# A graph layer with residual and layer norm on one Trainium2 core: pair counting of groups 1 to 3 regrouped from three turns to two, six pair places, the table word loaded inside the loop

## The reference

```python
agg = segment_sum(x[src], dst, num_segments=6250)          # 6250 x 256
h = relu(agg @ W_rel + b_rel + x @ W_root)                 # 6250 x 512
i, f, g, o = split(h @ W_ih.T + b_ih + b_hh, 4)            # f is not used
c = sigmoid(i) * tanh(g)
y = (sigmoid(o) * tanh(c)) @ W_fc + b_fc                   # 6250 x 256
out = layernorm(x + y)                                     # eps 1e-5
```

## Time and profile before

| | us |
|---|---|
| median of three runs | 1830.2 |
| profiled execution | 1824.41 |
| its span, first to last instruction | 1822.5 |
| TensorE matmuls busy | 1513.5 |
| GpSimd busy | 1281.0 |
| VectorE busy | 815.9 |
| ScalarE busy | 418.5 |
| mean granted TensorE clock | 0.91 of full |

### The profile page before, as it was taken

The page is one execution under the profiler, slowest core; times in us unless marked ns, Lnnn a source line. Parts: engine busy times, 40 slices in busy tenths (PEclk is TensorE's granted clock), DMA queues, the critical chain, the costliest instruction groups (busy, mean ns, idle before and its releaser), DMA issues.

```text
span 1822.5 us, 31499 instructions
## 1 busy us (share of the span) xinstructions
PE 1513.5 (83%) x6882; PEld 1213.0 (67%) x6883; DVE 815.9 (45%) x1763; ACT 418.5 (23%) x743; POOL 1281.0 (70%) x1926
## 2 busy tenths in 40 slices
PE   0157688697988898788998889899988888999997
PEld 0023355486767676667887667688876676888886
DVE  8877666431322654531324565422244654222332
ACT  0001021110112332220222333212223332222333
POOL 5875877777777877877777668776763668656640
PEclk9976677698988998889999999999998998999999
DMA  9563555576766555567766445576652455766540
GB/s 342 209 233 87 150 161 145 157 225 207 215 195 180 162 162 165 161 198 223 223 206 180 138 133 166 160 246 217 203 155 77 133 146 161 225 189 177 150 122 18
DMA packets 131966, 319.14 MB, mean 175 GB/s; under 512 B 17295, under 2 KB 68268, under 8 KB 130198
## 3 DMA queue, kind: packets, MB, share of 16 engines
q0 software_dynamic: 75264, 245.95, 46.4%
q10 hardware_dynamic: 52632, 54.80, 9.5%
q1 hardware_dynamic: 3936, 16.62, 2.4%
HBM read 298.10 MB, written 19.20 MB: 174 GB/s over the span
## 4 chain that ended last, share of the span: by engine, by line
PE 48%; POOL 21%; issue 19%; DVE 4%; DMA 3%; DVEq 3%; POOLq 1%; ACT 0%; ACTq 0%; SPq 0%
PE ps_blk L537 20%; POOL rows L400 14%; PE ps_agg L476 9%; PE ps_win L464 6%; POOL idx L370 6%; PE ps_y L545 4%; PE ps_blk L519 3%; PE ps_blk L524 3%; PE ps_tr L451 1%; DMA hot_key<-in_xb 1%; POOL rows L385 1%; PE ps_win L451 1%; DMA rows<-x_parts,idx 1%; POOLq L370 1%; DMA wih_sb<-in_x 1%
## 5 line engine op out<-in xcount | busy, mean ns | idle before, releaser
L400 POOL DMA_INDIRECT rows<-x_parts,idx x924 | 963.5, 1043 | 453.5 <-PE ps_agg L476 157.6
L537 PE MATMUL ps_blk<-cell,wih_sb 128*128 128x250 f32 x2400 | 545.5, 385 | 2.9 <-issue 2.2
L537 PEld LDWEIGHTS ps_blk<-cell,wih_sb 128*128 128x128 f32 x2400 | 464.1, 196 | 69.5 <-issue 8.8
L476 PE MATMUL ps_agg<-rows,onehot 128*125 x1112 | 341.8, 462 | 153.2 <-SPq L339 70.8
L476 PEld LDWEIGHTS ps_agg<-rows,onehot 128*125 128x125 f32 x1112 | 234.1, 216 | 227.5 <-issue 175.9
L906 DVE SCALAR_TENSOR_TENSOR onehot<-iota_f,tile_first,dst_u 128x500 f32 (+1 forms) x278 | 207.0, 746 | 291.7 <-PE ps_agg L476 171.6
L370 POOL COPY idx<-src_sb 128x1 int32 x956 | 264.4, 277 | 16.7 <-issue 9.7
L664 ACT ACTIVATE cell<-ps_blk,bg_sb 128x250 f32<-128x250 f32 x300 | 140.8, 470 | 544.0 <-PE ps_blk L537 470.2
L897 DVE TENSOR_TENSOR hot_key<-iota_h,rel 128x980 f16 x263 | 174.4, 663 | 0.4 <-issue 0.4
L464 PE MATMUL ps_win<-adj,hot_key 128*128 128x250 f32 x784 | 170.7, 375 | 2.4 <-DMA hot_key<-in_xb 1.5
L464 PEld LDWEIGHTS ps_win<-adj,hot_key 128*128 128x128 f32 x784 | 148.0, 190 | 21.6 <-DMA hot_key<-in_xb 4.0
(11 more groups left out here) (125 smaller groups left out, 914.2 us busy)
## 6 DMA issues: line engine op xcount, KB each, us to landing
hot_key<-in_xb ACTq DMA_DIRECT2D x28, 896.0 KB
rows<-x_parts,idx POOLq DMA_INDIRECT x924
x_t<-in_xT ACTq DMA_DIRECT2D x25, 250.0 KB
x_n<-in_x ACTq DMA_DIRECT2D x25, 250.0 KB
out<-y ACTq DMA_DIRECT2D x25, 250.0 KB
x_parts<-wih_sb SPq DMA_DIRECT2D x4, 1024.0 KB, 6.8
wih_sb<-in_x ACTq DMA_DIRECT2D x6, 512.0 KB, 9.7
x_parts<-cell SPq DMA_DIRECT2D x2, 1024.0 KB, 7.6
```

Of the source, the lines that this page charges most:

```text
L400: g.indirect_dma_start(rows_f[:, k * QC + j, :], None, x_parts, bass.IndirectOffsetOnAxis(ap=idx[:, k, j:j + 1], axis=0)).then_inc(landed[ ...
L476: ins = mm(o, onehot[:, hot * QC + j, 0:TN], rows[:, ds(slot + j, 1), :].squeeze(1), start=(first and j == 0), stop=False)
L537: last = mm(o, wih_sb[:, k, col:col + P], h_t[:, k, :], start=(k == 0), stop=(k == KH - 1))
```

## The change

`SLOTS` becomes (3, 3, 3, 3), so groups 1 to 3 are dealt as group 0 is: 3, 3, 3, 3 and 3, 3, 3, 4 windows in two turns. Turns 5 and 6 count group 1, 7 and 8 multiply, 9 is group 1; groups 2 and 3 follow in 10 to 14 and 15 to 19. Turn 20 sums the second tile of group 20, turns 21 to 24 are plain. Pair places are six instead of four, the table has one more (zero) word. The table word of the next span is loaded inside the pair loop of the present one; the first before all loops. Memory for the larger places comes from `src_sb`: the int32 sources now land in the last place of `rows` (`src_i`), VectorE makes a 16-bit copy `src_u` for GpSimd, and the first gather into that place waits until VectorE has read the int32 words (`src_read`).

```diff
--- before.py
+++ after.py
@@ -17,7 +17,7 @@
 GROUP_WINDOWS = GN // WN
 WINDOWS = DENSE * GROUP_WINDOWS
 SPANS = DENSE * GN // SN
-FIRST_SLOTS, SLOTS = (3, 3, 3, 3), (2, 2, 3, 2)
+FIRST_SLOTS, SLOTS = (3, 3, 3, 3), (3, 3, 3, 3)
 SRC_HI = -(-N_NODES // P)
 SCOLS = SN * SRC_HI
 WCOLS = WN * SRC_HI
@@ -32,7 +32,7 @@
 MAX_STEPS = TILES * (STEPS - 1) + 1
 MAX_VISITS = TILES * STEPS
 MAX_PAIRS = SPANS * STEPS
-PAIRS = 4
+PAIRS = 6
 QP, QPC = 98, 16
 RING = 7
 IDX_AHEAD = 1
@@ -55,7 +55,7 @@
 
 
 T_MORE_A, T_MORE_B, T_STEPS, T_GROUP0, T_SPAN = 0, 64, 128, 129, 160
-T_COLS = T_SPAN + SPANS
+T_COLS = T_SPAN + SPANS + 1
 PACK = 2048
 
 
@@ -148,7 +148,7 @@
         ident = sb("ident", [P, P])
         ones = sb("ones", [P, 1])
         zero_bf = sb("zero_bf", [P, 256], bf16)
-        src_sb = sb("src_sb", [P, CHUNK_COLS], i32)
+        src_u = sb("src_u", [P, CHUNK_COLS], u16)
         dst_u = sb("dst_u", [P, CHUNK_COLS], u16)
         src_lo = sb("src_lo", [P, CHUNK_COLS], f16)
         key = sb("key", [P, CHUNK_COLS], u16)
@@ -191,6 +191,7 @@
         flat = rows_f.rearrange("p r d -> p (r d)")
         dstq_sb = flat[0:QP, 0:QPC * CHUNK].bitcast(i32).rearrange("p (c e) -> p c e", c=QPC)
         dst_next = flat[0:QP, QPC * CHUNK:(QPC + 1) * CHUNK].bitcast(i32)
+        src_i = flat[:, (RING - 1) * QC * D_ROW:(RING - 1) * QC * D_ROW + CHUNK_COLS].bitcast(i32)
         cell_flat = cell[:, :, :].rearrange("p i n -> p (i n)")
         wih_flat = wih_sb[:, :, :].rearrange("p k n -> p (k n)")
         flat_a = adj[:, :, :].rearrange("p k n -> p (k n)")
@@ -240,6 +241,8 @@
 
         dstq_in = sem("dstq_in")
         edges_in = sem("edges_in")
+        src_short = sem("src_short")
+        src_read = sem("src_read")
         bias_in = sem("bias_in")
         weights_in = sem("weights_in")
         piece_in = [sem(f"piece_in{i}") for i in range(X_PIECES)]
@@ -294,9 +297,11 @@
         steps_begun = sem("steps_begun")
         stats_seen = sem("stats_seen")
 
-        def unpack(engine, regs, at):
+        def load_span(engine, regs, at):
+            engine.reg_load(regs[0], table[0:1, at:at + 1] if isinstance(at, int) else table[0:1, ds(at, 1)])
+
+        def unpack(engine, regs):
             packed, first, past = regs
-            engine.reg_load(packed, table[0:1, at:at + 1] if isinstance(at, int) else table[0:1, ds(at, 1)])
             engine.reg_alu(first, packed, PACK, ALU.python_divide)
             engine.reg_alu(past, first, -PACK, ALU.mult)
             engine.reg_add(past, past, packed)
@@ -314,7 +319,7 @@
         def _(sp):
             sp.dma_start(dstq_sb, dstq[0:QP * QPC * CHUNK].rearrange("(p c e) -> p c e", p=QP, c=QPC)).then_inc(dstq_in, 16)
             sp.dma_start(dst_next, dstq[QPC * CHUNK:(QP + 1) * QPC * CHUNK].rearrange("(p e) -> p e", p=QP)[:, 0:CHUNK]).then_inc(dstq_in, 16)
-            sp.dma_start(src_sb[:, :], srcT).then_inc(edges_in, 16)
+            sp.dma_start(src_i, srcT).then_inc(edges_in, 16)
             sp.dma_start(dst_i, dstT).then_inc(edges_in, 16)
             sp.sem_inc(gathered, RING)
             for i in SP_PIECES:
@@ -359,7 +364,7 @@
                 pool.wait_ge(piece_high, i + 1)
                 g.tensor_tensor(low, low, piece(i)[:, :, 0, :], ALU.subtract).then_inc(piece_split_pool, 1)
             pool.wait_ge(table_ready, 1)
-            pool.wait_ge(edges_in, 32)
+            pool.wait_ge(src_short, 1)
             steps = pool.value_load(table[0:1, T_STEPS:T_STEPS + 1], min_val=2 * TILES, max_val=MAX_STEPS)
             group0 = pool.value_load(table[0:1, T_GROUP0:T_GROUP0 + 1], min_val=0, max_val=2 * STEPS)
 
@@ -367,7 +372,7 @@
                 return pool.snap(((s + group0) % STEPS) * QC, min_val=0, max_val=(STEPS - 1) * QC)
 
             def copy_index(chunk, k, j):
-                g.tensor_copy(idx[:, k % RING, j:j + 1], src_sb[:, ds(chunk + j, 1)]).then_inc(idx_copied, 1)
+                g.tensor_copy(idx[:, k % RING, j:j + 1], src_u[:, ds(chunk + j, 1)]).then_inc(idx_copied, 1)
 
             for k in range(IDX_AHEAD):
                 chunk = chunk_of(pool.snap(0 * steps + k))
@@ -381,6 +386,8 @@
                     for j in range(QC):
                         pool.wait_ge(landed[ahead - RING][j], 16)
                 pool.sem_inc(steps_begun, 1)
+                if k == RING - 1:
+                    pool.wait_ge(src_read, 2)
                 for j in range(QC):
                     g.indirect_dma_start(
                         rows_f[:, k * QC + j, D_IN:D_ROW], None, x,
@@ -426,6 +433,7 @@
             place = pe.alloc_register("place")
             more_places = pe.alloc_register("more_places")
             pe.reg_mov(place, 0)
+            load_span(pe, pe_regs, T_SPAN)
             pe.reg_mov(step_0, 0)
             pe.reg_mov(visit_0, 0)
             pe.reg_mov(pair_0, 0)
@@ -442,7 +450,7 @@
                     for side in range(2):
                         at = w * 2 + (T_SPAN + side)
                         o = bank[:, side * SCOLS:(side + 1) * SCOLS]
-                        first, past = unpack(pe, pe_regs, at)
+                        first, past = unpack(pe, pe_regs)
                         with pe.Fori(first, past, QC):
                             s = pe.snap(pair_0, min_val=0, max_val=MAX_PAIRS)
                             half = pe.snap(place, min_val=0, max_val=PAIRS - 1)
@@ -450,6 +458,7 @@
                             for j in range(QC):
                                 last = mm(o, hot_lo[:, ds(half, 1), j // 2, :, j % 2].squeeze(1), hot_key[:, ds(half, 1), j // 2, :, j % 2].squeeze(1), start=False, stop=False)
                             last.then_inc(pairs_summed, 1)
+                            load_span(pe, pe_regs, at + 1)
                             next_pair(pe, pair_0, place, more_places)
                     marker(bank[:, 0:WCOLS]).then_inc(win_done, 1)
 
@@ -838,6 +847,8 @@
             link(v.tensor_scalar(row[:, BAD, 0:1], row[:, BAD, 0:1], 1.0, plain, ALU.add, ALU.mult))
             link(v.tensor_tensor(table[:, T_STEPS:T_STEPS + 1], row[:, BAD, 0:1], row[:, FLAG, 4:5], ALU.add))
             dve.sem_inc(table_ready, 1)
+            dve.wait_ge(edges_in, 32)
+            v.tensor_copy(src_u[:, :], src_i).then_inc(src_short, 1)
             split_pieces(POOL_PIECES, PARTS)
             count_below(SPANS, 2 * TILES + 1, (span_first[0:QP, :], span_end[0:QP, :]))
             dve.sem_inc(span_counts, 1)
@@ -855,12 +866,12 @@
             link(v.tensor_scalar(hi, hi, -float(QC - 1), None, ALU.add))
             link(v.scalar_tensor_tensor(table[:, T_SPAN:T_SPAN + SPANS], lo, float(PACK), hi, ALU.mult, ALU.add))
             dve.sem_inc(spans_ready, 1)
-            dve.wait_ge(edges_in, 32)
             v.tensor_copy(dst_u[:, :], dst_i).then_inc(setup, 1)
-            v.tensor_scalar(src_part, src_sb[:, :], P - 1, None, ALU.bitwise_and).then_inc(setup, 1)
-            v.tensor_scalar(src_high, src_sb[:, :], P.bit_length() - 1, None, ALU.logical_shift_right).then_inc(setup, 1)
-            n_setup[0] += 3
+            v.tensor_scalar(src_part, src_i, P - 1, None, ALU.bitwise_and).then_inc(src_read, 1)
+            v.tensor_scalar(src_high, src_i, P.bit_length() - 1, None, ALU.logical_shift_right).then_inc(src_read, 1)
+            n_setup[0] += 1
             dve.wait_ge(setup, n_setup[0])
+            dve.wait_ge(src_read, 2)
             link(v.tensor_copy(src_lo[:, :], src_part))
             link(v.tensor_scalar(wide, dst_u[:, :], float(DENSE * GN), float(SRC_HI), ALU.min, ALU.mult))
             link(v.tensor_tensor(key[:, :], wide, src_high, ALU.add))
@@ -874,6 +885,7 @@
             place = dve.alloc_register("place")
             more_places = dve.alloc_register("more_places")
             dve.reg_mov(place, 0)
+            load_span(dve, dve_regs, T_SPAN)
             step_0 = dve.alloc_register("step_0")
             visit_0 = dve.alloc_register("visit_0")
             pair_0 = dve.alloc_register("pair_0")
@@ -884,7 +896,7 @@
             def span(w, side):
                 at = w * 2 + side
                 static = isinstance(w, int)
-                first, past = unpack(dve, dve_regs, at + T_SPAN)
+                first, past = unpack(dve, dve_regs)
                 with dve.Fori(first, past, QC) as c:
                     s = dve.snap(pair_0, min_val=0, max_val=MAX_PAIRS)
                     half = dve.snap(place, min_val=0, max_val=PAIRS - 1)
@@ -893,6 +905,7 @@
                                     None, ALU.subtract).then_inc(rel_made, 1)
                     v.tensor_tensor(hot_lo[:, ds(half, 1), :, :, :].squeeze(1), iota_h[:, 0:P, :].unsqueeze(1).to_broadcast([P, PQ, P, 2]),
                                     src_lo[:, ds(c, QC)].rearrange("p (q c) -> p q c", c=2).unsqueeze(2).to_broadcast([P, PQ, P, 2]), ALU.is_equal)
+                    load_span(dve, dve_regs, at + (T_SPAN + 1))
                     dve.wait_ge(rel_made, s + 1)
```

## The result

The changed kernel takes 1893.95 us (median of 4 runs, 1893.18 to 1897.24), the one before 1828.11 (1822.73 to 1832.34): ratio 1.0358, 95% interval 1.0334 to 1.0383. It is 66 us slower. I forecast 1838.4 in a range of 1809 to 1862: the sign that I held likeliest, and far too small. The profiled execution after took 1893.3 us (span 1891.5, mean granted clock 0.889; before 1822.5 and 0.91).

What follows compares the result with a forecast made beforehand. TensorE and GpSimd were taken to bound the kernel in turns. Load +8.5, src words +1.0 and schedule -1.3 (including the six places) summed to +8.2 us: 1838.4 on the median of 1830.2, range 1809 to 1862.

Steps and rivals of the forecast that it cites:

- the sign that I held likeliest: Whole kernel: slower by more than the 9 us that can be told from no change; chance 0.42.
- part 2: Six pair places in the counting gaps: fewer late one-hots before the next sum, -3 us a turn, bounds 0 and -6.
- the clock: Counting turns, rival: denser gaps lower TensorE's clock, 2 us more per turn (12); chance 0.18 together with the end.
- Part 1, group 0: Table load inside the pair loop, group 0's first gap: 25 more loads at 0.34 us, +8.5 us.
- Part 1, groups 1 to 3: Table load moved from front to end of the counting gaps: zero, between +8 and -48 us.
- the faster rival: Counting gaps: pair supply was the bound, six places remove all late one-hots, another -18 us, 1820; chance 0.24.
- Part 3, the windows: Counting turns of groups 1 to 3: each added window costs 4.0 us, three in the first turn, four in the second.
- Group 1's product and dense turn: Group 1 after counting: 29 steps by 6.35 = 184, less some 5 the ring has ahead = 179 us.
- Part 4: Src words: conversion ahead of the first index copy +1.0 us; two-byte index copies zero, bounds -19 to +32 us.
- The end: Last plain turns: 119.2 to 256.7 us, +137.5; whole turns 41, 41, then GpSimd takes over, 46 and 50.
- the rival's +9: End, part of the clock-and-end rival: GpSimd the bound one turn earlier, +9 us; chance 0.18 together with the clock.
- The rival's sign: End, test for the clock-and-end rival (chance 0.18): the last four whole turns all take 47 us or more.

Runs made afterwards that it cites:

- e14: Kernel before with SLOTS (3, 3, 3, 3) alone, plus four 245-column matmuls of zeros behind every pair: 1844.8 us, ratio 1.0093.
- e6: Kernel before with four matmuls of zeros, 245 columns each, behind every pair: 1807.6 us, ratio 0.9902.
- e12: Changed kernel with one GpSimd index copy a step and four 245-column matmuls of zeros behind every pair: 1775.6 us, ratio 0.9712.
- e18: Kernel before with one GpSimd index copy a step and four 245-column matmuls of zeros behind every pair: 1706.8 us, ratio 0.9343.
- e10: Changed kernel with one GpSimd copy of four index columns a step instead of four one-column copies: 1806.1 us, ratio 0.9888.
- e2: Kernel before with only the table word loaded inside the pair loop: 1845.6 us, ratio 1.0104.
- e4: Changed kernel with the table load back ahead of each span's loop: 1878.5 us, ratio 1.028.
- e3: Kernel before with six pair places and the 16-bit src words, old plan and load: 1822.9 us, ratio 0.9992.
- e1: Kernel before with SLOTS (3, 3, 3, 3) alone, four pair places, load outside the loop: 1878.3 us, ratio 1.028.
- e9: Kernel before with one GpSimd copy of four index columns a step instead of four one-column copies: 1735.2 us, ratio 0.9495.

## Why the prediction was wrong

The schedule's mechanism held, its balance did not. I added -138.8 us for the three groups to +137.5 for the end and called it -1.3; the trace of the change has -89.4 and +148.7. The steps that failed are part 2, which took a slow array for late one-hots and booked -18 us that no run shows; the clock, left out of the sum and sized too small as a rival; the load of groups 1 to 3, put at nothing; and the turn at which GpSimd takes over at the end.

The ledger, by the ends of turns in the traces (us; negative is a saving):

| stretch | forecast | changed less before | plan alone, with filler (e14 less e6) | change, with copy and filler (e12 less e18) |
|---|---|---|---|---|
| to the end of group 0's own turn | +9.5 | +8.9 | -0.3 | +27.4 |
| group 1 | -54.2 | -35.8 | -45.5 | -28.1 |
| group 2, counting | -41.9 | -23.5 | -34.8 | -28.6 |
| group 3, counting | -42.7 | -30.1 | -28.2 | -26.7 |
| products and dense turns of 2 and 3 | 0 | +0.8 | +3.6 | +3.5 |
| the end | +137.5 | +148.7 | +148.2 | +124.1 |
| sum | +8.2 | +69.0 | +43.0 | +71.6 |

- **Part 1, group 0: right.** +8.9 for +9.5; GpSimd's first long wait ends at 162.64 (I wrote near 162), and from there its own pace hides the other loads. e10 and e12 show what stands there without that cover: 27 us.
- **Part 1, groups 1 to 3: wrong.** I took zero, between +8 and -48, on the argument that the front load ran anyway and the end load follows it. The upper end was nearer: what ran anyway at the front cost nothing, so moving it to the end is a new price, and it shows as the idle time ahead of the markers. e2 costs 20.6 us of which 9.5 are group 0's, after less e4 15.5 of which 7.5 are: 8 to 11 us, good to a few us.
- **Part 2: wrong, the largest term that was not there.** "I see up to 1.5 us of late one-hots a gap and take half": -3 a turn, -18 over six turns, and it was the base of the faster rival. e3 shows none alone, e4 against e1 none in the new plan. The 3.65 us for which VectorE stood on a place cost nothing, since the register steps set the gap's pace, and the 3.77 us were the lower clock. Twelve instead of eight matmuls in less time was the hint.
- **Part 3, the windows: right at the full clock.** First counting turns of e14 stand 12.8, 9.4 and 14.3 us above those of e6, for three windows by 4.0; the second ones 16.5, 16.9 and 18.1, for four. Group 1's product and dense turn are another matter: 184.2 us, where I had 179 after taking off 5 for steps that the ring would hold.
- **Part 4: right.** The first index copy starts at 33.0 us, 1.0 later. The copies' mean is 281 ns, in e3 even 297, and e3 is no slower than the kernel before.
- **The clock: right as a rival, too small and too unlikely.** I priced it at 12 us and gave it 0.18 together with the end. It took some 16. The sum went wrong where I took 67.4 and 69.7 us from turns at a clock of 0.87 and 0.93 and added windows at the same price, although three gaps of two windows became gaps of three in each.
- **The end: the schedule right, one turn off.** The gather is the bound in the turns of 46.0, 50.9 and 50.9, one turn earlier than I had it: +11, the rival's +9. The rival's sign as I gave it, four whole turns of 47 or more, did not come (40.6 and 46.0 are among them). e10 shows that it is the gather's pace: 41 to 42 us without it.

16 + 11 + 18 + 5 + (8 to 11) on my +8.2 gives 66 to 69 us, the 66 of the medians and the 69 of the profiles. That it closes so well is in part luck, since the 16 and the 8 to 11 are each good to several us only. Nor are these shares that can be taken off one by one: with clock and gather out of the way (e12 less e18) the change still costs 69 us, as other parts of it come uncovered. What stays in every pair is the exchange itself: what a group saves comes back as plain turns at the end, and at these sizes 24 to 46 us are saved for each turn that costs 41 to 50.

## What to carry to other kernels

Before a stretch is called late, look at the granted clock in it: long matmuls with no idle between them, at a granted clock of 0.50, are a slow array, not a late input. Work packed denser into gaps of register steps made the sums behind them dearer here; price the moved piece and what runs behind it. And where a schedule has a fixed number of turns, a turn taken out of the middle is worth only what its removal saves beyond the price of its twin at the end, where another engine may be the bound.

## What was not expected of the hardware

- Matmuls of zeros, which change no result, made the kernel before 1% faster (ratio 0.9902); the same number with one column made it 0.35% slower (1.0035, interval 1.0012 to 1.0058).
- On GpSimd an index copy of 128x4 takes as long as one of 128x1 (285 ns mean in e10, 281 in the changed kernel). One copy a step, behind the first gather, also takes away the 0.87 us wait for the last copy ahead of every step: the wait of the gathers on `idx` falls from 152.1 to 23.0 us in e9, and a step is 5.1 us in e10 (from the copy at 1661.8 to that at 1666.9), where 6.35 to 6.87 were counted in the kernel before. Copy and filler together give 1706.8 us, 6.6% under the kernel before, which neither the change nor its parts approach.
